# A two-layer pre-activation convolution kernel: one memory map for contraction, finish and layer 1, and the weights prepared on ScalarE

## The reference, cut to what matters

```python
# layer 0
x0 = gn(x)                                  # statistics over all tokens, 32 groups of 2 channels
xn = ln(x0)
left  = (xn @ left_w  + left_b)  * mask * sigmoid(xn @ lgate_w + lgate_b)
right = (xn @ right_w + right_b) * mask * sigmoid(xn @ rgate_w + rgate_b)
gate  = sigmoid(xn @ ogate_w + ogate_b)
out   = einsum('bkjd,bkid->bijd', left, right)      # one 512^3 product per channel
x1 = x + (ln(out) @ out_w + out_b) * gate
# layer 1: 12 x 12 lowest Fourier modes of gn(x1), mixed by complex weights, transformed back
y = x1 + irfft_modes(einsum('bcmn,comn->bomn', fft_modes(gn(x1)), w_real + 1j * w_imag))
```

## Time and profile before

| | us |
|---|---|
| median of 3 runs | 3029.33 (3028.93 to 3033.02) |
| the profiled execution | 3029.29 |
| its span, first to last instruction | 3027.5 |
| PE busy | 2510.4 (83%) |
| DVE busy | 2207.5 (73%) |
| ACT busy | 1372.8 (45%) |
| POOL busy | 1020.9 (34%) |
| mean granted TensorE clock | 0.946 of full speed |
| moved by DMA | 950.26 MB, 314 GB/s over the span |

### The profile page before, as it was taken

How to read it: one execution, slowest core, us unless ns; L and a number is a source line. 1 busy time by engine, 2 the same in 40 slices (tenths; PEclk the granted TensorE clock), 3 DMA queues, 4 the chain that set the end, 5 groups by cost and what they waited for, 6 DMA issues and landing times. The chain is left out here.

```text
span 3027.5 us, 40932 instructions
## 1 busy us (share of the span) xinstructions
PE 2510.4 (83%) x12694; PEld 1864.6 (62%) x12694; DVE 2207.5 (73%) x3463; ACT 1372.8 (45%) x1778; POOL 1020.9 (34%) x1042
## 2 busy tenths in 40 slices
PE   0008999889889979999999992989988988789775
PEld 0005666556556658888888881556655655588664
DVE  5998888778778748888888885766766766226453
ACT  0006888778778857666766671212211221100000
POOL 1018888778778800000000000444444444300000
PEclk9999999999999989999999996999999999769988
DMA  9845999788779767777777773999999999749999
GB/s 375 341 188 192 341 337 336 287 307 314 284 294 336 285 256 280 275 282 285 281 277 280 284 263 129 389 379 379 377 372 371 380 386 364 247 163 393 418 419 406
DMA packets 260650, 950.26 MB, mean 314 GB/s; under 512 B 31153, under 2 KB 31665, under 8 KB 260146
## 3 DMA queue, kind: packets, MB, share of 16 engines
q1 hardware_dynamic: 226160, 877.25, 76.7%
q10 hardware_dynamic: 34370, 71.54, 6.1%
HBM read 540.83 MB, written 407.90 MB: 313 GB/s over the span
## 5 line engine op out<-in xcount | busy, mean ns | idle before, releaser
L1104 POOL TENSOR_TENSOR fi_square_sum<-fi_square_sum,fi_square 128x1024 f32<-128x1024 f32 x128 | 302.7, 2365 | 429.0 <-ACT fi_square L1075 429.0
L780 PE MATMUL ct_acc_ps<-ct_l_hi,ct_r_hi 128*128 128x512 f32 x1024 | 404.3, 395 | 20.6 <-ACT ct_l_hi L794 20.6
L652 DVE SCALAR_TENSOR_TENSOR pj_lr<-pj_v_ps,layer_b_val,pj_sig 128x1024 f32<-128x1024 f32 x256 | 328.8, 1284 | 121.7 <-ACT pj_sig L589 118.4
L1075 ACT ACTIVATE fi_square<-fi_x 128x1024 f32<-128x1024 f32 x128 | 135.4, 1057 | 600.5 <-DVE fi_x L1132 590.9
L781 PE MATMUL ct_acc_ps<-ct_l_lo,ct_r_hi 128*128 128x512 f32 x1024 | 404.2, 395 | 0.0
L782 PE MATMUL ct_acc_ps<-ct_l_hi,ct_r_lo 128*128 128x512 f32 x1024 | 404.1, 395 | 0.0
L1031 PE MATMUL fi_y_ps<-fi_scaled,layer_w_bd 128*128 128x512 f32 x512 | 282.1, 634 | 71.1 <-DVE fi_scaled L1115 70.9
L490 POOL TENSOR_TENSOR front_ring<-front_ring,layer_gn_shift 128x512 f32<-128x512 f32 x256 | 333.5, 1304 | 5.5 <-DVE front_ring L618 5.5
L1115 DVE TENSOR_TENSOR fi_scaled<-fi_m,fi_s_ps 128x512 f32<-128x512 f32 x256 | 174.0, 680 | 190.5 <-DMA fi_m<-mixed_d 162.5
L589 ACT ACTIVATE pj_sig<-pj_g_ps,layer_b_gate 128x1024 f32<-128x1024 f32 x256 | 285.5, 1115 | 43.0 <-PE pj_g_ps L555 40.5
L1302 PE MATMUL la_ps_ps<-la_col,la_inv_cols 128*128 128x256 f32 x1024 | 243.3, 400 | 46.5 <-DVE la_early L1372 28.0
(11 more groups left out here) (183 smaller groups left out, 5035.8 us busy)
## 6 DMA issues: line engine op xcount, KB each, us to landing
lr_d<-pj_lr SPq DMA_DIRECT2D x128, 1024.0 KB, 5.8
gate_d<-pj_gout SPq DMA_DIRECT2D x128, 512.0 KB, 6.8
ct_l<-lr_d SPq DMA_DIRECT2D x64, 1024.0 KB, 7.1
ct_r<-lr_d SPq DMA_DIRECT2D x64, 1024.0 KB, 9.0
mixed_d<-ct_o SPq DMA_DIRECT2D x64, 1024.0 KB, 4.9
fi_m<-mixed_d SPq DMA_DIRECT2D x128, 512.0 KB, 14.1
fi_g<-gate_d SPq DMA_DIRECT2D x128, 512.0 KB, 12.9
fi_x<-in_x SPq DMA_DIRECT2D x32, 2048.0 KB, 9.1
```

The source lines that it names most:

```text
L652: dve.scalar_tensor_tensor(out=out[:, :, RG * (m % 2):RG * (m % 2) + RG], in0=v_ps[:, :].rearrange("p (q i) -> p q i", i=RG), scalar=keep. ...
L780: pe.matmul(bank, high, l_hi[b][:, :, k, :], start=(k == 0), stop=False)
L1104: pool.tensor_tensor(square_sum[:, :, :], square_sum[:, :, :], square[:, :, :], ALU.add).then_inc(sum_done, 1)
```

## The change

1. *prepare*: the weights are built on ACT in place of DVE, beside the statistics; DVE keeps two mask casts and the three low parts. Chunk 1 is taken by halves too. The 768 KB of `basis_rows` and the making of `pick` move to contract.
2. *One area of SBUF* (196 KB per partition) is shared by contract, finish and layer 1 (class Shared). So contract can load for finish: 4 `fi_g`, 5 tiles of x and 4 `fi_m`.
3. *contract*: the scale is worked out in two halves, the square of the mean goes to ACT and one product with the mask is dropped (the mask's square is made at the start by POOL). High and low parts go from SBUF to SBUF by 16 DMAs of 128 KB (spread_part); `scale_d` is gone.
4. *finish*: written out without loops. 5 x buffers; the store of a tile is issued after its last square (slot 1 of the next tile); the last 5 tiles are not stored and stay in SBUF. The load of tile k, still in slot 4 of tile k-2, waits for the store of tile k-5. Two PSUM banks for the Fourier sums. They go to memory in one DMA of 96 KB per tile and come back in 4 batches of 28 rows of 24 KB; those of the last 4 tiles go from SBUF to SBUF, one partition per DMA.
5. *layer 1*: no load of `fourier_d`. It begins with the 5 tiles that stayed, loads 3 more at the start and 2 when `la_col` is done; 10 buffers; stores are issued by ACT, loads by SP. The spectrum is cleared by POOL and DVE after the weight matmuls (the memory is in use until then).

```diff
 def prepare(nc, x, ins, tab, keep):
-        loads.append((keep.basis_rows[:, :, :], tab["t_basis_rows"]))
...
+            act.wait_ge(loaded, DMA * len(loads))
+            act.wait_ge(pool_set, 7)
+            copy(ow_scaled[:, :], ow[:, :], onw[:, 0:1])
+            copy(w_scaled[:, :, :], w_raw[:, :, :], nw[:, 0:1]).then_inc(scaled_ready, 1)
...
-                if i in (0, NCHUNK - 1):
+                if i in HALVED:
...
-            for i in range(2):
+            for i in range(3):
                 statistics(i)
...
+            for i in range(3, NCHUNK - 2):
+                statistics(i)
             for i, (w_high, w_low) in enumerate((keep.w_val, keep.w_gate, keep.w_og)):
-                link(dve.tensor_copy(w_high[:, :], w_full[:, i, :]))
+                dve.wait_ge(w_split, i + 1)
                 dve.tensor_tensor(w_low[:, :], w_full[:, i, :], w_high[:, :], ALU.subtract)
...
+            for i in range(NCHUNK - 2, NCHUNK):
                 statistics(i)
...
 def contract(nc, lr_d, mixed_d, basis_rows, keep, mid):
+        def spread_part(eng, part, source, e):
+            for q in range(RG):
+                rows = slice(P // 4 * q, P // 4 * q + P // 4)
+                at = P // 2 * part + P // 4 * e
+                eng.dma_start(mid.st[at:at + P // 4, q, :].bitcast(F32),
+                              source[rows, e, :, :].rearrange("p t j -> p (t j)").bitcast(F32)).then_inc(mid.s_loaded, DMA)
...
+                if isinstance(n, int) and n == C - 1:
+                    for c in range(MB):
+                        mid.load_gate(sp, c)
+                    sp.wait_ge(l_low, C)
+                    sp.wait_ge(r_low, C)
+                    for k in range(2):
+                        mid.load_x(sp, k)
                 sp.wait_ge(out_dve, n + 1)
                 sp.wait_ge(out_act, 3 * n + 3)
                 sp.dma_start(view[2][n], flat(om[b])).then_inc(stored[b], DMA)
...
+            sp.wait_ge(summed, WT * C)
+            mid.load_x(sp, 2)
             for b in range(2):
                 sp.wait_ge(stored[b], DMA * (C // 2))
+            for c in range(MB):
+                mid.load_mixed(sp, c)
+            for e in range(2):
+                sp.wait_ge(low_ready, e + 1)
+                spread_part(sp, 1, s_low, e)
+            for k in range(3, XT):
+                mid.load_x(sp, k)
...
 def finish_layer0(nc, x1_d, fourier_d, keep, mid):
+                k = n // TH + 2
+                if n % TH == 4 and XT <= k < TILES:
+                    sp.wait_ge(x1_stored[k % XT], DMA * (k // XT))
+                    sp.wait_ge(f_ready, k - XT + 1)
+                    sp.wait_ge(squared, TG * (k - XT) + TG)
+                    mid.load_x(sp, k)
+                k = n // TH - 3
+                if n % TH == 6 and inside(k, TILES) and k % BATCH == BATCH - 1 and through_memory(k):
+                    for b in range(2):
+                        sp.wait_ge(f_stored[b], f_count(k + 1, b))
+                    rows = slice(RG * (k + 1 - BATCH), RG * (k + 1))
+                    sp.dma_start(mid.rows[rows, :, :], rows_v[rows, :, :]).then_inc(rows_loaded, DMA)
...
+                    if g % TG == TG - 1 and k < KEPT:
+                        act.dma_start(x1_v[k], xt[k % XT].rearrange("p g t c -> p g (t c)")).then_inc(x1_stored[k % XT], DMA)
...
+                    if through_memory(k):
+                        act.dma_start(f_v[k], four[b].rearrange("p g c -> p (g c)")).then_inc(f_stored[b], DMA)
+                    else:
+                        for r in range(RG):
+                            act.dma_start(mid.rows[RG * k + r:RG * k + r + 1, :, :], four[b][M2 * r:M2 * r + M2, :, :]).then_inc(
+                                f_stored[b], DMA)
...
 def layer1(nc, x1_d, w_real, w_imag, inverse_rows, inverse_columns, out, keep, mid):
-            sp.dma_start(early[:, 0:M2 * WT * C], fourier_d.rearrange("p m r c -> p (m r c)")).then_inc(f_loaded, DMA)
...
+            for n in range(XT, FREE):
+                load(n)
+            sp.wait_ge(col_ready, C // CB)
+            for n in range(FREE, XR):
+                load(n)
+            for n in range(XR, NTG):
+                sp.wait_ge(stored[n % XR], DMA * (n // XR))
+                load(n)
...
+            for n in range(NTG):
+                act.wait_ge(y_done, WS // 2 * n + WS // 2)
+                act.dma_start(o_v[TILE[n]], by_group(xt[n % XR])).then_inc(stored[n % XR], DMA)
```

More of the change, by code:

```diff
@@ L799, in _ @@
             high(0, 0, 0)
+            act.dma_start(mid.basis_rows[:, :, :], basis_rows).then_inc(mid.basis_loaded, DMA)
             def square(n, b):
@@ L955, in finish_layer0 @@
-        block = ctx.enter_context(nc.Block())
-        def halves(eng, lead, slot):
-            for u in range(-lead, LOOP):
-                slot(u, u, 0)
-            with eng.Fori(1, HALVES // LOOP - 1) as j:
-                for u in range(LOOP):
-                    slot(LOOP * j + u, u, j)
-            for u in range(HALVES - LOOP, HALVES + 2 * TH + 4):
-                slot(u, u - (HALVES - LOOP), HALVES // LOOP - 1)
-        def is_int(n):
-            return isinstance(n, int)
-        def ahead_of(n, ahead, count):
-            return not is_int(n) or 0 <= n + ahead < count
+        rows_loaded = t.sem("rows_loaded")
@@ new lines, in finish_layer0, with halves, through_memory, f_count @@
+        rows_v = fourier_d.rearrange("n r m f -> (n r) m f")
+        f_v = fourier_d.rearrange("n r m f -> n (r m) f")
+        x1_v = x1_d.rearrange("n g p f -> n p g f")
+        block = ctx.enter_context(nc.Block())
+        def halves(lead, slot):
+            for n in range(-lead, HALVES + 2 * TH + 4):
+                slot(n)
+        def through_memory(k):
+            return k < TILES - DIRECT
+        def f_count(k, parity):
+            return sum(DMA if through_memory(i) else RG * DMA for i in range(k) if i % 2 == parity)
@@ L1021, in _, with spread @@
+            for n in range(HALVES):
+                slot(n)
+            sp.wait_ge(rows_loaded, DMA * ((TILES - DIRECT) // BATCH))
         @block.tensor
         def _(pe):
-            def spread(n, m, j):
+            def spread(n):
                 at_least(pe, m_scaled, n - 1)
                 part_of = st[:, n // (2 * P // 4), HW * (n % 2):HW * (n % 2) + HW]
-                pe.matmul(s_ps[n % 2], keep.pick[:, n // 2 % (P // 4), :], part_of, start=True, stop=True).then_inc(s_ready, 1)
-            def project_out(n, m):
+                group = n // 2 % (P // 4)
+                pe.matmul(s_ps[n % 2], mid.pick[:, group, :], part_of, start=True, stop=True).then_inc(s_ready, 1)
@@ L1091, in _ @@
+            halves(0, slot)
+            for b in range(XT):
+                act.wait_ge(x1_stored[b], DMA * len(range(b, KEPT, XT)))
             for b in range(2):
-                act.wait_ge(f_stored[b], RG * DMA * (GROUPS // TG // 2))
+                act.wait_ge(f_stored[b], f_count(TILES, b))
         @block.gpsimd
@@ L1144, in _ @@
+            halves(2, slot)
             link = chained(dve, step)
@@ L1164, in layer1 @@
     NTG = GROUPS // TG
-    XR = 5
+    XR = XT + 5
+    SPLIT_O = 40
+    FREE = XT + 3
+    KEPT = NTG - XT
+    TILE = [(KEPT + n) % NTG for n in range(NTG)]
     CB = L // GR
```

527 lines of the change are left out of this document (267 added, 260 removed).

## The result

| | us |
|---|---|
| after, median of 4 runs | 2902.83 (2902.22 to 2904.15) |
| before, beside it on the same chip, median of 4 runs | 3029.13 (3017.63 to 3033.02) |
| ratio, with its 95% interval | 0.9594 [0.9577, 0.961] |
| the profiled execution; its span | 2902.31; 2900.5 |

What follows compares the result with a forecast made beforehand. PE was taken to bound contract, memory the last stage, and SP's stall to slow finish, with memory next. Terms -13 - 21.5 - 56 - 18 - 26 = -134.5 from 3029.3 gave 2895 us, range 2862 to 2935.

Steps and rivals of the forecast that it cites:

- The 94 groups: Finish, groups 14 to 108: all four streams run, memory sets 5.21 us per group at 412 GB/s, 490 us.
- Rival A: Finish's mean rate stays at 383 GB/s, 690 us for the stage, a gain of 23; 2928 us in all, chance 0.2.
- rival B: PE alone bounds finish as memory keeps up, 614 + 10 us; 2862 us in all, chance 0.1.
- Front: Start of the kernel: chunk 1 by halves and weights off DVE end the statistics at 193.9 instead of 206.9, -13 us.
- passage to layer 1: From the last `fi_x` to layer 1's first matmul: 13.8 us instead of 31.8, without the load of `fourier_d`, -18 us.
- tiles: Layer 1's tiles, bound by memory: 24 loads and 32 stores take 284.5 us instead of 311.3, -27 us.
- Contract to finish: Passage from contract's end to the first `fi_scaled`: DVE starts at 1864.4 instead of 1885.9, -21.5 us.
- POOL has `pick` in contract, where it is idle: Part of the front step: making `pick` on POOL in contract; start of contract was predicted at 0 us.
- The clearing is 3.2 us on DVE and 4.3 on POOL beside 4.0 us of other steps: Layer 1's chain, clearing the spectrum after the weight matmuls; together with the weights' arrival, +1 us.
- The four row loads: Finish: loads of Fourier rows, 0.69 MB each, counted by bytes within 0.05 MB per group, 1.7 us each.
- Rival C: Finish: 28-partition row loads block SP's queue ahead of `fi_m`; at 60 us each 3075 us in all, chance 0.02.
- The signs: Listed trace observations; wrong if `fi_m` waits exceed 100 us, finish windows fall under 390 GB/s, or 20 us intervals surround row loads.

Runs made afterwards that it cites:

- Experiment 4: The changed kernel with each x tile's store put back to two slots before the load that waits for it; median 2940.98 us, ratio 0.9734 to before.
- experiment 10: The changed kernel with one row load of 112 partitions in place of four of 28, where the last stood; median 2886.11 us, ratio 0.9545 to before.
- experiment 1: The changed kernel with POOL making `pick` only after DVE's first two low parts; median 2894.85 us, ratio 0.9583 to the kernel before.
- experiment 2: The changed kernel with ACT instead of POOL clearing part of the spectrum (36 channels, DVE 28); ratio 0.9602 to the kernel before.

## Why the prediction was right, and where it wasn't

**The bounds.** Finish was held up by the order on SP's queue, with full DMA and PE's 4.80 us close behind, and that is how it came out: 416 GB/s in its middle, and 653.9 us against 657. The 94 groups in which all streams run took 493.1 us, 5.25 each, against 490 and 5.21; the other 34 and the start took 160.8 against 167. (The prediction's 713 us for the stage before is a slip: 1885.94 to 2600.5 is 714.6.) Experiment 4 gives 37 of the 61 us back when the store alone is moved. Rival A (383 GB/s is all that the mix gives) falls with the windows of 416 and with experiment 10; rival B (PE alone) was not reached, yet finish without three of the row loads, 638 us, is closer to its 624 than to the forecast. The rule of about 358 GB/s from the Trainium skill (DMA: Bandwidth & Descriptors, Specifications), which spoke against the forecast, would have made finish 730.

**Front, passage to layer 1, tiles.** -12.4, -18.1 and -26.7 against -13, -18 and -27. The replay of the chunks gave chunks 2 to 6 at 68.8, 89.2, 111.3, 131.8 and 153.8, and the last statistics at 193.9; DVE began them at 68.80, 89.21, 111.68, 132.08 and 153.91, and ended at 193.85. The last weight table landed 25.9 us after its issue, which is 26.5 after layer 1's first matmul; forecast 26. The page's list of issues after (KB each, median us to landing):

```profile
x_d<-fi_x ACTq DMA_DIRECT2D x27, 2048.0 KB, 14.0
la_w<-in_L_conv_w_imag SPq DMA_DIRECT2D x1, 2304.0 KB, 25.9
fi_s<-ct_s_high ACTq DMA_DIRECT2D x8, 128.0 KB, 4.4
fi_s<-ct_s_low SPq DMA_DIRECT2D x8, 128.0 KB, 3.5
```

**Contract to finish**, -19.0 against -21.5. Here the size of one term was off: the issue of a small DMA on SP was taken as 0.44 us and was 0.83. Why is open: the one at 1852.98 took 0.84 us too, when ACT's queue had been done since 1851.5.

**What failed** is two sentences with the same mistake. "POOL has `pick` in contract, where it is idle" looked at POOL's time alone; what the work covers it with is DVE's, and it cost 6.3 us on the chain (experiment 1). "The clearing is 3.2 us on DVE and 4.3 on POOL beside 4.0 us of other steps" added up two engines as if they ran side by side; they did not, and of the +5.9 against +1 this is 3.2 (experiment 2). The rest is 1.0 us by which the clearing on two engines that don't collide is still longer than the steps of before (5.0 and not 4.0 us), 0.8 between the last copy of the spectrum and the first tile (16.69 us for the matmuls of `la_col`, 15.93 before), and 0.9 of waiting for the last weight table, of which the forecast had 0.4. The chain that ended last shows this wait:

```profile
2526.73 25.90 DMA la_w<-in_L_conv_w_imag
...
2552.67 31.91 PE la_ps_ps L1357 x288
```

**The four row loads** were "in the 0.05 MB", and three of them cost 5 us each and not 1.7. It didn't show in the sum, since finish's other terms were high by more: without these three the 94 groups take 477.3 us, 5.08 each (experiment 10), and the forecast's 490 less their 5 us is 485. That the middle of finish came out at 493 for 490 is luck. So is a part of the 2902.8 against 2895: +6.9, +4.9 and +2.5 that the forecast lacked stand beside -4.7 in finish and -2.9 in project.

**Rival C** (the row loads block the queue) had the right place and a price some nine times too high (45 us each). **The signs**: "waits for `fi_m` still over 100 us" was to show the forecast wrong, and was met (123.0) though the forecast held. It watched the engine with time to spare; PE's own wait, 26.9 us, was the one to name. "Windows under 390 GB/s in finish" were met too, in the 20 us with 363 behind a row load. Project's -2.9 us was in no step, and no run explains it; traces of the same project code differ by as much (869.8 to 872.8 us).

## What to carry to other kernels

An instruction moved to an idle engine is free only if no engine on the chain shares something with it: look at what VectorE does in the same microseconds before GpSimd is given work over SBUF. In a stage with full DMA, count transfers by the share of engine time and not by bytes: copies into one partition cost some ten times their bytes there, and a transfer that can wait belongs in a stretch where the DMA engines have time, as the one row load at the end of finish. And read the idle stretches that end on "issue" in a loop, whatever the change at hand: here four of them were worth more than any passage that the change shortened.

## What the runs showed of the hardware that was not expected

- GpSimd holds VectorE up until its own instruction ends: four instructions that take 2.74 us together took 8.94 beside a GpSimd operation that reads SBUF, and a copy from SBUF to SBUF of 0.23 us took 3.99 beside a GpSimd clearing. A copy out of PSUM was not held (0.69 us with and without).
- A turn of VectorE's loop cost 9.1 us of its own time and some 12 us of the stage.
- A copy of 24 KB into one partition cost 0.42 us of a stage with full DMA, about 0.6 when the row loads that it replaces are allowed for; 24 KB are worth 0.06 at 416 GB/s.
- SP needed 0.83 us to issue a DMA of 128 KB into 32 partitions, and 0.43 us for loads of 512 KB in the kernel before.
- One core moved 416 to 421 GB/s for stretches of 100 us, loads and stores mixed.
